# A two-layer attention and FFN kernel on one core: K ahead of Q in the opening, a bank of its own for Q, three of the first norms later, and in the tail another split between VectorE and ScalarE

## The reference

```python
x = x + xattn0(layernorm(x), ctx, Wq, Wk, Wv, Wo, bo)    # 16 heads of 64, softmax over 375
x = x + ffn0(layernorm(x), gate_w, w1, b1, w2, b2, sw1, sb1, sw2, sb2)  # top-1 of 2 experts + shared
x = x + attn1(layernorm(x), ctx, ctx, mask)              # one head of 256, masked rows
x = x + ffn1_int8(layernorm(x), W_int8, W_scale, bias)
# ffn1_int8: x_scale = max(|x2|).max() / 127 over ALL tokens of all batches;
#            x_int8 = clip(round(x2 / x_scale)); (x_int8 @ W_int8.T) * x_scale * W_scale + bias
```

## Time and profile before

| what | value |
|---|---|
| median of 3 runs | 918.49 us (918.43 to 918.54) |
| profiled execution | 917.72 us, span 916.0 us |
| TensorE busy | 894.1 us, 98% of the span |
| VectorE, ScalarE, GpSimd busy | 65%, 59%, 29% |
| chain that ended last | 93% TensorE, 5% VectorE |
| opening without TensorE work | 0 to 9.9 us |
| after the last matmul | 911.7 to 916.0 us |

### The profile page before, as it was taken

The page is one execution under the profiler, slowest core; times in us unless marked ns, Lnnn a source line. Parts: engine busy times, 40 slices in busy tenths (PEclk is TensorE's granted clock), DMA queues, the critical chain, the costliest instruction groups (busy, mean ns, idle before and its releaser), DMA issues.

```text
span 916.0 us, 19720 instructions
## 1 busy us (share of the span) xinstructions
PE 894.1 (98%) x6719; PEld 788.9 (86%) x6719; DVE 595.5 (65%) x1603; ACT 537.8 (59%) x1285; POOL 262.3 (29%) x354
## 2 busy tenths in 40 slices
PE   5999999999999999999999999999999999999997
PEld 4888888998888898888898888987898999998776
DVE  6678766666666666665666666666764666438767
ACT  4666555555565556555565565666572455356875
POOL 1344234324343343342343343244100000023200
PEclk9999999999999999999999999999999999999999
DMA  9313000000000000000000000000252043355522
GB/s 278 104 41 110 1 19 22 7 17 5 17 5 22 17 5 17 5 22 17 5 17 5 17 13 13 1 6 7 100 184 87 1 132 130 110 140 178 167 69 81
DMA packets 29501, 50.24 MB, mean 55 GB/s; under 512 B 2960, under 2 KB 24112, under 8 KB 27680
## 3 DMA queue, kind: packets, MB, share of 16 engines
q1 hardware_dynamic: 27920, 45.97, 16.1%
q0 software_dynamic: 1536, 3.67, 1.4%
HBM read 41.37 MB, written 8.26 MB: 54 GB/s over the span
## 4 chain that ended last, share of the span: by engine, by line
PE 93%; DVE 5%; ACT 1%; issue 1%; DMA 1%; POOL 0%; DVEq 0%
PE bank L1871 28%; PE bank L1900 10%; PE bank L2116 9%; PE bank L2028 9%; PE bank L1919 9%; PE bank L1885 8%; PE bank L1940 5%; PE bank L1844 4%; PE bank L2203 2%; PE bank L2221 2%; PE bank L1853 1%; PE bank L2080 1%; PE bank L1817 1%; PE bank L2210 1%; DVE neg_max L1300 1%
## 5 line engine op out<-in xcount | busy, mean ns | idle before, releaser
L773 POOL TENSOR_TENSOR probs<-probs,row_rcp 112x375 f32<-112x375 f32 x256 | 209.2, 840 | 389.6 <-DVE row_rcp L1306 388.2
L899 ACT ACTIVATE probs<-bank,neg_max 112x375 f32<-112x375 f32 x256 | 144.2, 569 | 55.0 <-DVE neg_max L1300 54.7
L1900 PE MATMUL bank<-ident,probs 112*125 112x112 f32 x768 | 129.1, 278 | 1.8 <-DVE probs_t L1311 1.8
L1300 DVE TENSOR_REDUCE neg_max<-bank 112x1 f32<-112x375 f32 x256 | 123.3, 539 | 10.3 <-PE bank L1885 10.1
L1900 PEld LDWEIGHTS bank<-ident,probs 112*125 112x125 f32 x768 | 113.5, 187 | 18.6 <-issue 3.7
L1311 DVE COPY probs_t<-bank 125x336 f32<-125x336 f32 x128 | 64.7, 506 | 60.7 <-PE bank L1900 56.7
L871 ACT ACTIVATE k_parts<-bank 128x376 fp32r<-128x376 f32 x128 | 62.0, 485 | 67.6 <-PE bank L1871 67.6
L1871 PE MATMUL bank<-ctx_hi,down_hi 128*128 128x376 f32 x256 | 96.8, 378 | 0.6 <-DVE k_parts L1291 0.3
L874 ACT ACTIVATE v<-bank 125x512 f32<-125x512 f32 x96 | 57.5, 599 | 63.5 <-PE bank L1871 63.5
L1291 DVE TENSOR_TENSOR k_parts<-bank,k_parts 128x376 fp32r<-128x376 f32 x128 | 69.8, 546 | 29.9 <-ACT k_parts L871 28.8
L1919 PEld LDWEIGHTS bank<-probs_t,v 125*64 125x64 f32 x1536 | 74.0, 137 | 16.2 <-issue 16.0
(11 more groups left out here) (239 smaller groups left out, 1994.6 us busy)
## 6 DMA issues: line engine op xcount, KB each, us to landing
ctx_raw<-in_ctx_t SPq DMA_DIRECT2D x16, 375.0 KB, 3.4
stage<-in_ffn_up SPq DMA_DIRECT2D x5, 1024.0 KB, 5.0
stage<-in_ffn_down SPq DMA_DIRECT2D x5, 1024.0 KB, 6.9
ring_late<-in_ctx_t SPq DMA_DIRECT2D x10, 375.0 KB, 10.2
ring_late<-in_ctx_n SPq DMA_DIRECT2D x10, 375.0 KB
routed<-xn SPq DMA_DIRECT2D x1, 2240.0 KB, 9.5
rows_in<-routed SPq DMA_DIRECT2D x5, 448.0 KB, 6.3
answers<-y_rows SPq DMA_DIRECT2D x10, 224.0 KB, 2.7
```

Source lines behind the costliest of these rows:

```text
L773: eng.tensor_tensor(probs[s][:, :], probs[s][:, :], row_rcp[:, s:s + 1].broadcast_to([S, C]), ALU.mult).then_inc(probs_ready, 1)
L899: eng.activation(probs[r][:, :], SCORE_BANKS[i][0:S, 0:C], ACT.Exp, bias=neg_max[:, r:r + 1], accum_out=row_sum[:, r:r + 1]).then_inc(exp_ ...
L1300: eng.tensor_reduce(neg_max[:, r:r + 1], SCORE_BANKS[k][0:S, 0:C], AX.X, ALU.max, negate=True) \
L1900: t = eng.transpose(turn_bank(i, project)[0:CJ, j * S:(j + 1) * S], probs[QUAD * v + i][:, j * CJ:(j + 1) * CJ], ident[0:S, 0:S])
```

## The change

In words: (1) x of batch 0 is loaded alone, the other three batches of its group behind Wv left. (2) TensorE turns the identity matrix 22 times ahead of its first work. (3) Wk left is split in two parts of 256 columns, and the first two K units wait for the first part only. (4) The units' order is K1, K2, Q, K3, K4, V, with Q in bank 2. (5) On VectorE the norms of batches 1 to 3 stand behind the last K rest and ahead of the rests of Wk right and Wv right. (6) In the tail ScalarE takes the first root before the centred rows of batches 12 to 15 and also forms that of batch 15, which VectorE no longer does. (7) `out_scale` moves from GpSimd to VectorE, behind group 1's `quantise`. (8) The last `xi_t` is copied by VectorE, between `add_answers(0)` and `add_answers(1)`, not by ScalarE.

```diff
@@ SyncE
-            eng.dma_start(x_all[:, 0:GB, :], x[:, 0:GB, :]).then_inc(x_loaded[0], 16)
+            eng.dma_start(x_all[:, 0:1, :], x[:, 0:1, :]).then_inc(first_loaded, 16)
             eng.wait_ge(consts, 1)
             eng.dma_start(ctx_raw[:, :, 0:C], ctx_t[0]).then_inc(ctx_loaded, 16)
             load_piece(0)
             load_wq(0)
             load_piece(1)
+            eng.dma_start(x_all[:, 1:GB, :], x[:, 1:GB, :]).then_inc(x_loaded[0], 16)
@@ units: banks and counts
+        class Opening(Units):
+            q_bank = 2
...
+            def count(self, k):
+                return {K_UNIT + 1: 1, Q_UNIT: 2}.get(k, Units.count(self, k))
+            def frees(self, k):
+                return {Q_UNIT: 0, K_UNIT + 3: 1}.get(k, self.count(k) - 1)
@@ ScalarE
             round_ctx(0, 0)
-            piece_hi(0)
+            eng.wait_ge(half_loaded[0], 16)
+            eng.activation(wk_hi[:, :, 0:WK_PART], PIECES[0][3][:, :, 0:WK_PART], ACT.Copy).then_inc(wk_part_hi, 1)
+            eng.activation(wk_hi[:, :, WK_PART:512], PIECES[0][3][:, :, WK_PART:512], ACT.Copy).then_inc(weights_hi, 1)
             tokens_out(0, 0, heads_bank[0])
+            opening = Opening()
+            unit(opening, K_UNIT, 0, 0)
+            unit(opening, K_UNIT + 1, 0, 0)
             piece_hi(1)
-            opening = Units(0, 0)
-            for k in range(4):
-                unit(opening, k, 0, 0)
+            unit(opening, Q_UNIT, 0, 0)
+            unit(opening, K_UNIT + 2, 0, 0)
+            unit(opening, K_UNIT + 3, 0, 0)
             piece_hi(2)
...
-            for t in range(B - 5, B - 1):
-                centre(t)
+            centre(B - 5)
             eng.wait_ge(abs_zeroed, 2)
-            for cols in (slice(0, B - 4), slice(B - 4, B)):
+            last_root(slice(0, B - 4))
+            for t in range(B - 4, B):
+                centre(t)
+            last_root(slice(B - 4, B))
...
             answers_out(1)
-            xi_out(NG - 1)
             answers_out(NG - 2)
@@ VectorE
-            norm_batches(norm1, 2 + NORM_OPS, 1, GB - 1)
-            opening = Units(0, 0)
-            unit_lo(opening, 0, 0, 0)
-            unit_lo(opening, 1, 0, 0)
+            opening = Opening()
+            unit_lo(opening, K_UNIT, 0, 0)
+            unit_lo(opening, K_UNIT + 1, 0, 0)
             piece_lo(1)
-            for k in range(2, V_UNIT):
-                unit_lo(opening, k, 0, 0)
+            unit_lo(opening, Q_UNIT, 0, 0)
+            unit_lo(opening, K_UNIT + 2, 0, 0)
+            unit_lo(opening, K_UNIT + 3, 0, 0)
+            eng.wait_ge(x_loaded[0], 16)
+            batch_moments(norm1, 2 + NORM_OPS, 1, GB - 1)
+            batch_roots(norm1, 2 + NORM_OPS, 1, GB - 1)
             piece_lo(2)
             piece_lo(3)
...
-            eng.tensor_scalar(centred[(B - 1) % CENTRED], x_all[:, B - 1, :], norm4.moments[:, B - 1, 0:1], None,
-                              ALU.subtract).then_inc(last_centred, 1)
...
                 quantise(i)
+                if i == 1:
+                    eng.tensor_scalar(out_scale[:, :], ws_col[:, :], x_scale[:, 0:1], None, ALU.mult) \
+                       .then_inc(out_scale_ready, 1)
...
-            for i in range(NG):
+            add_answers(0)
+            eng.wait_ge(xi_turned, NG)
+            eng.wait_ge(acc_ready, KT * (NG - 2))
+            eng.tensor_copy(xi_t[(NG - 1) % 2][:, :, :], bank_b[(NG - 1) % 2][:, 0:KT * GT]
+                            .rearrange("p (k t) -> p k t", k=KT)).then_inc(last_xi_ready, 1)
+            for i in range(1, NG):
                 add_answers(i)
@@ TensorE
             eng.wait_ge(consts, 2)
+            for _ in range(22):
+                eng.transpose(TURN_BANK[:, 0:P], ident[:, :], ident[:, :])
             turn_tokens(0, 0, heads_bank[0])
-            opening, closing = Units(0, 0), Units(B - 2, 3)
+            opening, closing = Opening(), Units(B - 2, 3)
+            eng.wait_ge(wk_part_lo, 1)
+            unit(opening, K_UNIT, 0, 0, 0)
+            unit(opening, K_UNIT + 1, 0, 0, 0)
             eng.wait_ge(wq_loaded[0], 16)
-            unit(opening, 0, 0, 0, 0)
+            eng.wait_ge(xn_t_ready[0], 1)
+            unit(opening, Q_UNIT, 0, 0, 0)
             eng.wait_ge(weights_split, 1)
-            for k in range(K_UNIT, V_UNIT):
-                unit(opening, k, 0, 0, 0)
+            unit(opening, K_UNIT + 2, 0, 0, 0)
+            unit(opening, K_UNIT + 3, 0, 0, 0)
```

More of the change, by code:

```diff
@@ L450, in build_program @@
         class Units:
+            q_bank = 0
             def __init__(self, pair, r):
@@ L464, in count @@
                 return self.before[1] + (k + 1) // 2 + (1 if self.queries == 2 else 0)
+            def frees(self, k):
+                return self.count(k) - 1
             def hi_count(self, k):
@@ L509, in queries @@
         def queries(f, k, odd):
-            psum = bank[k % 2][:, 0:PAIRS * S]
             if f.queries == 1:
-                return (psum.rearrange("p (a s) -> p a s", a=PAIRS),
+                return (bank[f.q_bank][:, 0:PAIRS * S].rearrange("p (a s) -> p a s", a=PAIRS),
                         lambda parts, part: parts[:, part, :, odd * S:(odd + 1) * S])
             first = 2 * (k - PAIR_UNIT)
-            return psum.rearrange("p (a s) -> p a s", a=2), lambda parts, part: parts[:, part, first:first + 2, :]
+            return bank[k % 2][:, 0:PAIRS * S].rearrange("p (a s) -> p a s", a=2), lambda parts, part: parts[:, part, first:first + 2, :]
         def turn_bank(i, project):
             return TURN_BANK if project or i % 2 == 0 else bank[0]
+        WK_PART = 256
         PIECES = []
@@ L949, in _ @@
             round_ctx(0, 0)
-            piece_hi(0)
+            eng.wait_ge(half_loaded[0], 16)
+            eng.activation(wk_hi[:, :, 0:WK_PART], PIECES[0][3][:, :, 0:WK_PART], ACT.Copy).then_inc(wk_part_hi, 1)
+            eng.activation(wk_hi[:, :, WK_PART:512], PIECES[0][3][:, :, WK_PART:512], ACT.Copy).then_inc(weights_hi, 1)
             tokens_out(0, 0, heads_bank[0])
+            opening = Opening()
+            unit(opening, K_UNIT, 0, 0)
+            unit(opening, K_UNIT + 1, 0, 0)
             piece_hi(1)
-            opening = Units(0, 0)
-            for k in range(4):
-                unit(opening, k, 0, 0)
+            unit(opening, Q_UNIT, 0, 0)
+            unit(opening, K_UNIT + 2, 0, 0)
+            unit(opening, K_UNIT + 3, 0, 0)
             piece_hi(2)
-            unit(opening, 4, 0, 0)
+            unit(opening, V_UNIT, 0, 0)
             piece_hi(3)
-            for k in range(V_UNIT, 8):
+            for k in range(V_UNIT + 1, 8):
                 unit(opening, k, 0, 0)
@@ L1229, in norm_op, with batch_moments @@
                 o.then_inc(norm.step, 1)
-            def norm_batches(norm, base, first, n):
+            def batch_moments(norm, base, first, n):
                 for b in range(first, first + n):
@@ L1237, in norm_batches, with batch_roots @@
                     norm_moments(norm, b)
+            def batch_roots(norm, base, first, n):
                 for i in range(NORM_OPS):
@@ L1852, in unit @@
                             col = (PAIRS * cf + p) * P
-                            m = eng.matmul(bank[0][:, p * S:(p + 1) * S], wq_sb[:, kt, col:col + P],
+                            m = eng.matmul(bank[f.q_bank][:, p * S:(p + 1) * S], wq_sb[:, kt, col:col + P],
                                            xn_t[:, kt, bf, :], start=(kt == 0), stop=(kt == KT - 1))
```

46 lines of the change are left out of this document (28 added, 18 removed).

## The result

The changed kernel took 921.8 us in the median of 8 runs (919.45 to 922.4), the kernel before beside it 918.6 (917.8 to 920.5); the ratio is 1.0027, interval [1.0017, 1.0037]. Predicted were 915.0, a range of 914.0 to 918.7, and "faster"; it is 0.27% slower, which is small but clear of the noise. The profiled execution of the change took 921.97 us, its span is 919.8.

A forecast was written before the change was run, and what follows sets the result against it. TensorE holds 93% of the chain, but the change touches the first 30 us and last 25, where other engines share it. Opening -3.3 and tail -0.2 sum to -3.5 us: 915.0 from 918.49, range 914.0 to 918.7.

The forecast's parts named there:

- the first sentence on the clock: Opening, TensorE: the 22 identity turns start at 1.8 us, when GpSimd's identity is ready, and last until 6.8.
- the part on `out_scale` (7): Tail: forming `out_scale` on VectorE costs 0.1 us (0.07 to 0.2) on the chain, ahead of group 3's ratios.
- the rivals: Four alternatives: no clock rise on turns, 0.14; small first-load gain, 0.06; clock low all opening, 0.04; faster, 913.8, 0.02.
- the wait for VectorE: Opening: VectorE is late at the first row maximum, turning 2 us of TensorE's possible gain into a wait.
- The first rival: Opening: the clock does not rise on identity turns, K and Q run slow; 918.7 us, no change; chance 0.14.
- T: Start of the first K matmul in the opening, expected at 9.0 us, own range 8.5 to 9.7.
- Landing of x: Opening: batch 0's x, 112 KB, takes 2.8 us in proportion to size and lands at 3.6; bound 2.9.
- First row maximum at T+13.45: Opening, VectorE: the first row maximum starts 13.45 us after T, not at T+11.4 when the scores are ready.
- K unit 2 of the second half at T+17.1: End of the opening, TensorE: this unit starts 17.1 us after T, at 26.1 instead of 29.43.
- Opening: Start of the kernel up to K unit 2 of the second half: a gain of 3.3 us.
- From there the same distances: After the opening: all engines go on in their old distances, with the next loads still hidden.
- Tail: End of the kernel: 0.3 us gained by dropping VectorE's centring, 0.1 lost to `out_scale`, 0.2 gained in sum.

The follow-up runs named there:

- e2: The kernel before with only `out_scale` moved from GpSimd to VectorE, so the all-reduce ends GpSimd's list; 920.1 us, ratio 1.0023.
- e9: e1 with 8 more identity turns on TensorE between batch 0's turn and K; 913.2 us, ratio 0.9957.
- e1: The change plus one small GpSimd multiplication, its result unread, behind the last all-reduce; 913.9 us, ratio 0.9964.
- e3: The change without the 22 identity turns; 917.9 us, ratio 0.9992.
- e4: e1 without the 22 identity turns; 916.2 us, ratio 0.9988.
- e5: The change with the tail of the kernel before (parts 6 to 8 undone); 914.4 us, ratio 0.9964.
- e12: e1 with 11 identity turns in place of 22; 915.1 us, ratio 0.9978.
- e7: e1 with Wv right's rest and batch 1's xn formed later, behind K rests of the second half; 912.8 us, ratio 0.9946.
- e8: e1 with the roots of batches 1 to 3 and batch 1's xn moved to the second visit; 914.1 us, ratio 0.9961.
- e11: e7 and e9 together: Wv right's rest later and 8 more identity turns ahead of K; 912.2 us, ratio 0.9943.
- e6: The kernel before with parts 6 to 8 and e1's added GpSimd instruction; 916.7 us, ratio 0.9988.

## Why the prediction was wrong, step by step

**The step that failed** is the first sentence on the clock: "The 22 identity turns start when the identity is ready, 1.52 + 0.29 = 1.8 us". I took that time unchanged from before; it came out as 10.35. The term was missing from the part on `out_scale` (7): I counted what the move costs VectorE and not what it leaves as GpSimd's last instruction. The earlier trace rows held the warning, 6.85 us of "issue" ahead of an operation of 0.85; I used that row for when `out_scale` ended and didn't ask what the wait was. None of the rivals had it. By e2 this part alone costs the kernel before 2.1 us; in the change, where 22 turns and K are queued behind the identity, it costs 6.9 by the rows (32.15 against 25.26) and 0.63% by the ratios, 5.8 us.

**A size that was off: the wait for VectorE.** It was predicted as 2 us and measured 1.80 to 1.85, but I had counted its length only. In the change and in e9 the clock fell in it, 1.5 and 1.2 us more; in e1, e3, e4, e5 and e12 it didn't. My rivals looked at the clock at the start alone.

**Another size: the low clock at the start.** The first rival priced it at 3.7 us (K unit 2 of the second half at T+20.8 in place of T+17.1). Without the turns, or with 11, it came at T+18.06 (e3), T+18.47 (e4) and T+19.00 (e12), against T+16.86 in e1: 1.2 to 2.1 us.

**What held**, read in e1, where the reload is out of the way:
- Landing of x: 3.6 predicted with 2.9 as the bound; 2.94 in e1, 2.79 to 2.98 over all profiles with the new opening. 112 KB took 2.11 us, as long as the 1.8 KB of the earlier trace rows: in proportion to size was the wrong end. T was 8.40, 5.46 behind the landing where 5.35 were predicted, and by the early landing just outside my 8.5 to 9.7. In e4, e7, e8 and e11 Wk's landing bound K instead, as the prediction allowed, and T was 9.28, 8.67, 8.60 and 8.66.
- The clock rises on turns alone: K at a pitch of 0.17 in e1 and in the change, 0.31 in e4 and e12. The first rival falls, and the rule of the Trainium skill behind it (TensorE: Matmul & The Clock Gate, Part 4: PE-mode transpose) doesn't hold for these turns: e1 and the change measure the contrary, and in e8 to e11 the turns themselves become faster on the way (22 in 4.20 to 4.44 us, in e1 4.95).
- First row maximum at T+13.45: T+13.33 in the change, T+13.37 in e1. K unit 2 of the second half at T+17.1: T+16.83 and T+16.86. VectorE's queue could be summed up from the rows of before to 0.3 us.
- Opening: 3.3 predicted, 3.3 measured by the times (e5, 2.1 to 4.5). That the two agree is in part luck. By the rows K unit 2 of the second half came 4.2 us earlier (25.24 in e5, 29.43), since T was 0.6 below my 9.0. "From there the same distances" held as far as 57 us (the turn of a batch's tokens at 56.94 in e5, 61.14 before), but at the last moments 3.6 were left (889.44, 893.07). The rest went between 820 and 837 us before, in a stretch of an FFN: two of ScalarE's `hid` instructions stand at 820.67 and 836.13 before and at 816.47 and 832.54 in e5. Why isn't known; e1 and e6 lose 0.8 and 0.5 between the same two, the change nothing.
- Tail: 0.2 predicted; 0.56 by the rows. Taking the centring away gave 0.45, not 0.3, since the three maxima now follow the moments without any gap. The copy of `xi_t` took 0.62, near the lower end and not 1.1: it reads bf16, and the row that I priced it by was an addition in fp32. TensorE's queue covered it.
- The sum without the reload: 3.5 predicted; e1 3.3 us (2.1 to 4.6).

So by the ratio the time forecast was right for e1, a kernel that differs from the change by one unread instruction of GpSimd; its median, 913.86, lies 0.1 below the range.

## What to carry to other kernels

An instruction that is moved away also leaves something behind: look at what is now the last one on its engine, and whether the next execution starts in the state that it finds today. A long wait marked "issue" ahead of a tiny operation is a cost that has a place, and a move can bring it to a worse one; if a GpSimd library operation such as the all-reduce would be the last, put a cheap ordinary one behind it. And a wait of 1 to 2 us on TensorE is priced at its own length and, in some executions, again at what the lower clock takes from the work behind it.
